# One fused kernel of four residual blocks: key sums two convolutions behind, residual summed by TensorE, attention's bulk work one gap ahead, flag product four slots ahead, nodes scaled per quarter

## The reference

```python
x = x + L0(gn(x))   # 1x1 conv; depthwise 3x3, 5x5, 7x7 with gelu, gated and summed to ctx_all;
                    # global mean; k = softmax(key conv); qk = sum(ctx_all * k); small MLP; ctx_all + v
x = x + L1(gn(x))   # deformable convolution: value = 1x1; depthwise 3x3; offsets and masks = 1x1;
                    # 9 taps sampled bilinearly, weighted by the mask, 1x1
x = x + L2(gn(x))   # graph layer: each row scaled by d = exp(m_ii - logsumexp(m_i)), relu
x = x + L3(gn(x))   # sign of x against sign of the weights, 3x3 convolution
```

## Time and profile before

| | us |
|---|---|
| three runs | 341.95, 344.35, 344.81 (median 344.35) |
| the profiled execution | 341.88 |
| its span in the profile | 340.2 |
| VectorE busy | 285.6 (84%) |
| TensorE busy | 282.0 (83%) |
| ScalarE busy | 160.4 (47%) |
| GpSimd busy | 110.1 (32%) |
| mean granted TensorE clock | 0.945 of full speed |

### The profile page before, as it was taken

One profiled execution on the slowest core, in us unless ns is written; L12 is line 12 of the kernel. 1 busy time (PEld: TensorE's weight loads), 2 busy tenths in 40 slices (PEclk: granted clock), 3 DMA queues, 4 the chain that ended last, 5 costly groups with the idle time before them and its releaser, 6 DMA issues.

```text
span 340.2 us, 5922 instructions
## 1 busy us (share of the span) xinstructions
PE 282.0 (83%) x2202; PEld 169.6 (50%) x2202; DVE 285.6 (84%) x424; ACT 160.4 (47%) x258; POOL 110.1 (32%) x129
## 2 busy tenths in 40 slices
PE   8687959307899997999998969568889988995696
PEld 8336936207374443566664624565333443354672
DVE  5799999699949789999986657774999999998754
ACT  1499522220243858600000000597988888999200
POOL 3006898700430066999997006000000000000000
PEclk9999989856999999999999999759999999999599
DMA  3411000000000000000000000353000000000703
GB/s 127 146 54 34 9 9 2 0 0 2 1 2 0 0 0 0 2 2 2 2 0 2 2 1 0 123 125 123 3 0 0 0 0 0 0 3 0 119 7 123
DMA packets 7613, 8.71 MB, mean 26 GB/s; under 512 B 2212, under 2 KB 5796, under 8 KB 7588
## 3 DMA queue, kind: packets, MB, share of 16 engines
q1 hardware_dynamic: 6260, 7.20, 7.2%
q10 hardware_dynamic: 1328, 1.18, 1.6%
HBM read 4.18 MB, written 2.10 MB: 18 GB/s over the span
## 4 chain that ended last, share of the span: by engine, by line
PE 39%; DVE 20%; POOL 15%; issue 12%; ACT 11%; ACTq 3%; DVEq 0%; POOLq 0%
POOL arena L558 10%; PE ps L1462 8%; PE ps L1246 8%; PE ps L1233 7%; PE ps L1265 3%; PE ps L1347 3%; POOL arena L546 3%; ACT arena L787 2%; PE ps L1528 2%; PE ps L1442 2%; ACT arena L770 2%; ACT arena L623 2%; DVE stats L833 2%; POOL turns L558 2%; ACTq L347 2%
## 5 line engine op out<-in xcount | busy, mean ns | idle before, releaser
L1462 PE MATMUL ps<-arena 128*128 (+1 forms) x256 | 63.5, 380 | 6.8 <-ACT arena L770 5.9
L770 ACT ACTIVATE arena<-ps 128x2048 f32<-128x2048 f32 x32 | 60.1, 1878 | 8.3 <-PE ps L1462 8.3
L1462 PEld LDWEIGHTS ps<-arena 128*128 (+1 forms) x256 | 24.3, 97 | 41.4 <-issue 15.3
L616 ACT ACTIVATE rstd<-mv,eps 128x2 f32<-128x2 f32 x6 | 1.8, 296 | 90.7 <-DVE mv L836 86.5
L1117 DVE TENSOR_TENSOR arena<-arena 128x1024 f32 (+3 forms) x34 | 36.9, 1152 | 4.7 <-ACT arena L770 4.4
L1265 PE MATMUL ps<-ident 128*128 128x128 f32 x210 | 33.5, 334 | 7.3 <-DVE arena L1161 5.8
L1058 DVE TENSOR_TENSOR turns<-arena,ps 128x1024 f32<-128x1024 f32 x30 | 35.2, 1213 | 3.7 <-PE ps L1361 3.6
L558 POOL TENSOR_TENSOR arena<-arena 128x768 f32<-128x768 f32 x21 | 37.6, 1826 | 0.2
L1233 PE MATMUL ps<-turns,k 128*128 128x512 f32 x80 | 34.8, 594 | 2.4 <-DVE turns L1068 2.1
L1265 PEld LDWEIGHTS ps<-ident 128*128 128x128 f32 x210 | 32.4, 247 | 8.6 <-DVE arena L1161 6.0
L1134 DVE TENSOR_TENSOR arena<-arena 128x1024 f32<-128x1024 f32 (+13 forms) x30 | 32.6, 1152 | 0.5
(11 more groups left out here) (228 smaller groups left out, 484.9 us busy)
## 6 DMA issues: line engine op xcount, KB each, us to landing
scratch_x<-xs SPq DMA_DIRECT2D x4, 256.0 KB
arena<-arena SPq DMA_DIRECT2D x2, 512.0 KB, 3.3
out<-arena SPq DMA_DIRECT2D x4, 256.0 KB, 2.1
sN<-in_bias_n SPq DMA_DIRECT2D x48, 0.0 KB
xs<-in_x SPq DMA_DIRECT2D x8, 64.0 KB
xs<-in_x ACTq DMA_DIRECT2D x8, 64.0 KB
arena<-arena SPq DMA_DIRECT2D x4, 128.0 KB, 3.9
arena<-arena ACTq DMA_DIRECT2D x4, 128.0 KB, 4.4
```

What stands on the lines that cost most here:

```text
L770: act.activation(E[k], ps[:, (k % 2) * 2048:(k % 2 + 1) * 2048], ACT.Exp, scale=0.5 / SPLIT ** 2, accum_out=rowsum[:, bass.ds(i, 1)]).then ...
L1462: ins = pe.matmul(bank(b0 + q), w, m[:, bass.ds(i * P + 512 * q, 512)], start=(t == 0), stop=(t == 1 and q > 0))
```

## The change

- Weight spreads: the innermost dimension of the access patterns is changed, so that the band is read contiguously and the written elements lie 64 apart. The same numbers are written.
- GpSimd waits for the 7x7 weights of VectorE (`wt7_late`) in place of the 5x5 ones.
- `key_values` runs two parts behind the convolutions; after the last convolution come 14 warm-ups, the key sums of part 2, the global mean, and the last key sums.
- Each piece of bulk work in the attention stands one gap earlier; the first one stands before the wait for `kv_done`.
- x and the context are summed by TensorE in PSUM banks 4 to 7, as matmuls with the identity; ScalarE adds v as a bias when it writes x back.
- `values(1)` runs behind the depthwise part of L1, in place of 12 warm-ups; half of the turned values and some banks are moved accordingly.
- The flag's sum is taken at slot 12, its matmul at slot 18, its test at slot 21.
- Nodes are scaled per quarter on VectorE; ScalarE does one quarter in place of two (of which each is four instructions), and the warm-ups of the tail are split, begin earlier and write another bank. The mean product of the second half stands inside the first sign convolution.

```diff
-                ins = eng.tensor_scalar(view(wt, 16 * b, [(64, 8 * k), (1, HW)]), view(band, 0, [(1, 8 * k), (8 * k, HW)]),
+                ins = eng.tensor_scalar(view(wt, 16 * b, [(1, HW), (64, 8 * k)]), view(band, 0, [(8 * k, HW), (1, 8 * k)]),
                                         mask4[:, b:b + 1], None, ALU.mult)
...
-                eng.tensor_scalar(view(wt, c4hi * 4 * k * 64 + 16 * b, [(64 * k, 4), (64, k), (1, HW)], 64 * gp, 64),
-                                  view(band, gp * k, [(2 * k, 4), (1, k), (8 * k, HW)], 64 * c4hi, 64),
+                eng.tensor_scalar(view(wt, c4hi * 4 * k * 64 + 16 * b, [(1, HW), (64 * k, 4), (64, k)], 64 * gp, 64),
+                                  view(band, gp * k, [(8 * k, HW), (2 * k, 4), (1, k)], 64 * c4hi, 64),
...
-            pool.wait_ge(sem("wt5_ready"), 1)
+            pool.wait_ge(sem("wt7_late"), 16 - WT7_ACT)
...
+            def add_context(nq):
+                act.wait_ge(sem("x1_summed"), nq + 1)
+                for c2 in range(C2):
+                    act.activation(xs[:, nq * 512 + c2 * PX:nq * 512 + (c2 + 1) * PX], bank(4 + nq)[:, c2 * PX:(c2 + 1) * PX],
+                                   ACT.Identity, bias=vaddN[:, (2 * nq + c2) * HW:(2 * nq + c2) * HW + 1]
+                                   ).then_inc(sem("x1_ready"), 1)
+            act.wait_ge(sem("vadd_turned"), 1)
+            for nq in range(3):
+                add_context(nq)
+            root(rstd[:, 0:2], view(mv, 1, [(2, 2)]))
+            add_context(3)
+            root(rstd[:, 2:4], view(mv, 5, [(2, 2)]))
...
             for h in range(2):
-                group_norm(xh1, "xhat1", add_context, 2 * h, 2)
+                group_norm(xh1, "xhat1", lambda q: dve.wait_ge(sem("x1_ready"), 2 * q + 2), 2 * h, 2)
...
-                if l == 2 and t:
-                    key_values(t - 1)
-            key_values(QUADS - 1).then_inc(sem("kv_done"), 1)
+                if l == 2 and t > 1:
+                    key_values(t - 2)
+            warm_up(14, 6)
+            key_values(QUADS - 2)
             pe.wait_ge(sem("gelu"), 12)
             pe.wait_ge(sem("means_ready"), 2)
+            pe.wait_ge(sem("rows3"), QUADS)
             pe.matmul(bank(0, P), mean256, view(ctx_all, PX, [(SLOT, G), (1, HW)]), start=True, stop=True).then_inc(sem("glob_done"), 1)
+            key_values(QUADS - 1).then_inc(sem("kv_done"), 1)
...
+            def residual(nq, src, first):
+                ins = pe.matmul(bank(4 + nq), ident, src[:, nq * 512:(nq + 1) * 512], start=first, stop=not first)
+                if not first:
+                    ins.then_inc(sem("x1_summed"), 1)
...
-            warm_up(16)
+            for nq in range(2, NQ):
+                pe.wait_ge(sem("ctx_turned"), nq + 1)
+                residual(nq, ctxs[0], False)
+            warm_up(20, 0)
...
             pe.wait_ge(sem("dw_bias"), 2)
-            warm_up(12, 0)
+            values(1)
             pe.wait_ge(sem("dw_bias"), G)
...
                 accumulate(p, 0)
+                if p + LEAD == 20:
+                    pe.wait_ge(sem("over_rows"), 1)
+                    pe.matmul(bank(5)[0:1, PX:PX + 1], oversum, ones[:, 0:1], start=True, stop=True).then_inc(sem("over_all"), 1)
                 if p + LEAD < SLOTS:
                     build_slots(p + LEAD)
-                elif p + LEAD == SLOTS:
-                    pe.wait_ge(sem("over_rows"), 1)
-                    pe.matmul(bank(5)[0:1, 0:1], oversum, ones[:, 0:1], start=True, stop=True).then_inc(sem("over_all"), 1)
...
-            scale_nodes(1, 4)
+            scale_nodes(1, 0, 1)
             for q in range(4):
+                if q < 3:
+                    scale_nodes(1, q + 1, 1)
+                dve.wait_ge(sem("o2_ready"), q + 1)
                 add_back(1, q)
...
-            pe.wait_ge(sem("x3_ready"), 4)
-            warm_up(24)
+            pe.wait_ge(sem("col_summed"), 5)
+            warm_up(14, 4)
+            for quarter in (2, 4, 6, 8):
+                pe.wait_ge(sem("x3_ready"), quarter)
+                warm_up(8, 4)
             pair_means(1)
-            warm_up(12)
+            warm_up(10, 4)
...
+                    if (i, t) == (0, 4):
+                        pair_means(0)
```

113 lines of the change are left out of this document (60 added, 53 removed).

## The result

The changed kernel took 331.46, 331.52, 331.44 and 333.09 us, median 331.49; the kernel before, run beside it, 341.95, 344.35, 344.81 and 343.18, median 343.76. The ratio is 0.966 with a 95% interval of 0.962 to 0.970, so it is faster, by 10.4 us between the two profiled executions (341.88 and 331.46; spans 340.2 and 329.3).

The account below looks back on a forecast made before the run. VectorE up to about 94 us, then the last slots and the tail were taken as what edits can shorten; terms summing to 7.4 us saved gave 334.5, with run spread 335.7, range 333 to 338.5 (wider 331.5 to 341).

Parts of the forecast that it names:

- Spreads, GpSimd, keys: First-block convolutions: cheaper spreads, GpSimd's later start and later key sums bring the last context reduction 3.4 us sooner.
- 4.0 us comes back: VectorE's context work: GpSimd's later large products stretch two-input products, returning 4.0 us (0 to 4.1) of 6.7 gained.
- Rival (b): GpSimd and VectorE in the convolutions: collision milder than 1:1, up to 4 us better, 332; chance 0.10.
- Keys two behind: End of the convolutions: results no longer queue behind key sums, removing VectorE's 0.91 us idle before the last reduction.
- Bulk work: Attention: first gated product fills VectorE's wait for the key sums, leaving seven of eight pieces in the chain; 1.1 saved.
- Residual: Attention: eight context additions leave VectorE for TensorE and ScalarE; 2.1 us saved up to the transposes of x.
- Rival (c): Attention: TensorE at half clock through the residual matmuls, 1.7 us on v1 and v2; 338.9, chance 0.16.
- Rival (d): TensorE from warm-ups to depthwise: clock stays at 1.2 GHz until the values, ending 15 us late; 350.7, chance 0.06.
- Values: Around the depthwise part: values(1) behind it ends 0.3 us after the maps could start; 0.3 lost.
- Clock of the depthwise part: Depthwise part after TensorE's idle gap: half clock would lose 1.7 us; between 0 and 1.7, 0.9 lost was taken.
- Flag: Last slots: moving the flag's product and test to earlier slots removes VectorE's wait before the last sum; 0.9 saved.
- Rival (a): Weight spreads: the strided write is as dear as the strided read was; 338.3, chance 0.20.

Follow-up runs that it names:

- both experiments: Changed kernel with the spreads' old access pattern restored, ratio 0.974; changed kernel with GpSimd's large products again starting after the wt5 spreads, ratio 0.974.
- keys-one-behind profile: Changed kernel with key sums one convolution behind again and without the 14 warm-ups ahead of the last ones; ratio 0.975 to the kernel before.
- the experiment: Changed kernel with the flag's product and test before the last slot again and nodes scaled in the old pieces; median 334.18 us, ratio 0.974.

## Why the prediction was right, and where it was not

- *Spreads, GpSimd, keys, forecast -3.4, measured -4.4.* The mechanism (GpSimd's collision moved from the spreads to products that lose less) held in both experiments. The term "4.0 us comes back" was mis-sized: 2.2 did. I had taken one row where VectorE lost nearly the whole length of a GpSimd operation for the rule; with several in a row the loss is shared. Rival (b), "milder than 1:1", was the right one in kind, but that its 332 is the time that came out is luck: its condition gave 1.8 us of its 4, and the rest came from other terms. The gain of a small spread was priced rightly (0.12 each against 0.13). The start of the context work was forecast 6.7 sooner and was 5.85: 0.4 was lost in front of the 640-element spreads, which started 1.26 sooner and not 1.7, and they gave 0.54 and not 0.8. The prediction's own figures do not quite close here: 4 x (0.872 - 0.60) is 1.1 and not 0.8, and 6.7 - 4.0 is 2.7 and not 2.5.
- *Keys two behind, forecast 0.9 of those 3.4.* The step "with the keys two behind, convolution results no longer queue behind key sums" failed as a cause: VectorE's wait of 0.91 went with the keys as they were, because VectorE came sooner. Alone on the kernel before, the part removes that wait and makes the one at the copy longer by as much.
- *Bulk work, -1.1 against -1.8.* By order 1.23, and 0.6 by the links that the change drops; the second was in the diff and not in my sum. Undone alone the order is worth 1.9, since it also covers TensorE's residual matmuls.
- *Residual, -2.1 against -2.3.* As worked out. Rival (c), half clock through it, did not come in the changed kernel (0.92 granted), and its price does not hold for the first of these matmuls: in the keys-one-behind profile they ran at a granted 0.50, and the transposes of x started at 81.58 all the same. Rival (d), a lasting 1.2 GHz, is excluded in every profile.
- *Values, +0.3 against +0.31.* The maps start 8.66 behind the start of the depthwise part where they started 8.36 behind it, as worked out. What the sum left out is that both halves ahead of the depthwise part would by now hold it up by 0.7: with the part undone the maps are 0.46 later, so in this kernel it is a gain.
- *Clock of the depthwise part, +0.9 against 0.* The bounds 0 and 1.7 were right, the value between them was not a state the chip has: it was 0 in the profile of the changed kernel and 1.68 in five of eight with such a gap. The mean over these eight, 1.05, is near what I took, yet no profile is there. That the changed kernel's profile, and by their times three of its four runs, drew the fast value is luck, worth 0.9 against the forecast.
- *Flag, -0.9 against -1.28* (1.2 by the experiment), *tail, -1.1 against -1.44.* Both mechanisms as worked out, both a little larger; in the tail only as long as the transfers land early.
- Rival (a), a write as dear as a read, fell for VectorE: the pattern is worth 2.2 us. Its sum was off as well: it left 0.8 to 0.9 of the first stretch, and 2.21 is left with the pattern undone (copy at 61.71 against 63.92). The rule of the Trainium skill, "SBUF — State Buffer", section "Door 1: The DMA port swizzle", that a penalty falls at each new 16-byte line, would have left no gain; by the rows above the spreads with a strided write hold VectorE 17 to 30% less long than those with a strided read. Four of 640 elements take 2.53 us, 0.63 each; four contiguous rows of 512 take 2.0, which is 0.63 for 640 if it scales. At that size the write's stride costs VectorE nothing that shows.

Added up, the forecast for the profiled execution was 334.5 and 331.46 came. Of the 3.0 between them 1.0 is the first stretch, 0.7 the bulk work, 0.9 the clock of the depthwise part, 0.4 the flag, 0.3 the tail, 0.2 the residual; 0.5 went the other way outside the span. The 1.2 added for the spread of the runs was not needed either, as three of four lie within 0.1 of the profiled one.

## What to carry to other kernels

When one engine's stall is to be removed, look at who made it late: an edit that brings the other engine forward may remove the same stall, and two edits that share it do not add up. Moving a GpSimd operation pays by what it lies beside afterwards (nothing lost beside transposes; of VectorE's time 3.7 us beside one-input spreads and 2.2 beside two-input products here), not by how long it is. And where TensorE idles 2 to 4 us ahead of dense work, a few useless matmuls in the gap are worth trying: the starts behind them moved by about 0.1 us here, the depthwise part was fast in both profiles with its gap filled (three of eight with it open), and with all gaps filled five of six runs agreed within 0.2 us. The sixth did not, so something else still varies.

## What the hardware showed unexpectedly

- TensorE's clock after a short idle was not fixed by the instructions around it: in two kernels with the same TensorE instructions for 30 us before, at the same microsecond, a gap of 2.6 us was followed by a granted 1.00 in one profile and by 0.54 to 0.61 for 4 us in the other; one of 2.11 us by 7.11 and by 8.80 us for the same 16 matmuls; one of 3.77 us by 6.90 and 8.27 us for the same 96. Such a place is worth 1.2 to 1.7 us here. The Trainium skill, "TensorE: Matmul & The Clock Gate", section "HAM oscillation", tells of clocks that fall in idle gaps; that the same gap does it in some executions and not in others is what these profiles add.
- A one-input VectorE spread that started behind a large GpSimd product ended 0.42 us after it, both times (2.25 us against 0.60 on average, the products 2.08 and 2.12 us), while 32 x 32 transposes take 1.04 to 1.12 us each in all three profiles looked at, beside such products or not.
